# Softmax attention with another order of scores, maxima and values over two blocks of keys, and its first stacked rows fetched in four parts

## The chip, the cores and the metric

The kernel runs on one core of one Trainium2 chip. The metric is the device time of one execution in microseconds. Before the change, three executions took 3766.29, 3769.75 and 3779.08 us; the median is 3769.75 us.

## The reference, cut to what matters

The program is a network of six parts over x of shape (2, 2048, 256): a routed feed-forward part, a causal linear attention, the same feed-forward again, a feed-forward with 4-bit quantised operands, a softmax attention, and the quantised feed-forward again. Only the softmax attention is touched:

```
x = x + _L1_attn_ref(_layernorm(x, axis=-1), L1_attn_W_qkv, L1_attn_W_o)

b, n, _ = x.shape                     # 2, 2048, 256; 16 heads of 16
qkv = (x @ W_qkv.T).reshape(b, n, H, DH).transpose(0, 2, 1, 3)
score = softmax(einsum('bhif,bhjf->bhij', qkv, qkv) / 4, axis=-1)
attn = einsum('bhij,bhjf->bihf', score, qkv)
out = attn.reshape(b, n, F) @ W_o.T
```

Query, key and value are the same projection. Every row of scores has 2048 keys, and there are 2 x 16 x 2048 such rows.

## The kernel before, in words

The softmax attention is the function `attn1` (line 1492). Every engine walks through one generator, `plan()` (line 1554), that yields steps in one order, and does of each step its own share: TensorE (PE) the products, ScalarE (ACT) the exponentials and copies, VectorE (DVE) the maxima, normalisation and divisions, SyncE (SP) the DMAs. So the order of `plan()` is the order in which each engine issues, and an engine that waits for one step holds up all its later ones.

**Units and blocks.** A unit `u` is one batch row, one group of four heads and 512 queries; there are 32 (`UNITS`), four to a group of heads. Within it the loop `jt` goes over 16 blocks of 128 keys. Per block, `score` (line 1720) multiplies keys by queries for each of the four heads: a product of 50 rows into a ring of three PSUM banks `st`. Heads 0 and 2 lie on partitions 0 to 49 and heads 1 and 3 on 64 to 113, so that neighbouring products can use different halves of PE's rows. ACT takes the exponential (line 1796) into `PR`, a ring of two blocks. Score `s` waits until the exponential of `s - 2`, counted from one, is done: that is the one three places before it. The step `pv` (line 1734) multiplies the four exponentials of a block by the values, into bank `po`. It is issued one block late.

**Maxima.** A softmax needs the row's maximum first. The step `max` (line 1701, `m` in the order) computes scores with queries on the partitions, 48 rows, alternately on the two halves, into one of four spare banks, and DVE reduces it (line 1836). A unit has 64 of them (`MPU`), and they run 16 (`LEAD`) ahead of the unit's scores, so that unit `u + 1`'s last maxima fall in block 11 of unit `u`. Then the step `extremes` follows: DVE reduces once more (line 1843), PE transposes (line 1708), DVE splits into two parts (lines 1851 and 1853), and SP writes them out and reads them back as two more rows of the queries' tile `QS` (lines 1652 and 1656). The unit's first score waits for that.

**The order in a block** is the list `ORDER` (line 1508): `m s0 s1 m s2 v m s3 m`. After it come, outside the list:
- in block 0, `end` of the last unit: ACT copies `po` (line 1803), for which the first `pv` of the new unit waits, in block 1;
- in block 1, `tail` of the last unit: four transposes on PE (line 1742), and on DVE a reciprocal and a product (lines 1860 and 1864);
- from block 1 on, one step of `aside` per block. For units 1 to 4 these are the projection steps of the second batch row, 14 for each 512 rows: `norm` (DVE, line 124) and `turn` (PE transposes, line 1676, which wait for `norm`) four times by turns, `parts` twice (lines 1683, 1782, 1828) and `value` four times (line 1690);
- from block 2 on, one step of `put` per block, in the seven units 13 to 16 and 29 to 31: `ao` (PE transposes, line 1749, then an ACT copy, line 1811) and `wo` (line 1757, which waits for that copy, then DVE adds to x and takes the row's statistics), four times by turns.

**The start.** `project_steps(0)` projects the first batch row in four groups of 512 rows. Each group's parts go to DRAM (`q_parts`, line 1632). When all are there, the step `stack` (line 1640 on) reads them back as the stacked rows `KS` and `QS` of the first four heads, with 12 DMAs of 256 KB, and the first maximum waits for all of them. Stacks 1 to 7 are fetched in the same way while earlier units run. Before the first score come 80 steps `max`.

Of the kernel before, what the change touches and what calls it, by code (L numbers as in the profile page):

```python
# [6 lines left out]
F32 = mybir.dt.float32  # L7
# [49 lines left out]
def build_program(nc, A):  # L57
# [3 lines left out]
    TB = L // P  # L61
# [8 lines left out]
    DH = D // NH  # L70
    GT = 4
    G = T // GT
    GW = GT * P
# [5 lines left out]
    with ExitStack() as ctx:  # L79
        known = {}  # L80

        def event(name, by=1):
            if name not in known:
                known[name] = Event(ctx.enter_context(nc.semaphore(name)), by)
            return known[name]
# [1406 lines left out]
        def attn1():  # L1492
            with ExitStack() as scope:
                NPT = 3
# [3 lines left out]
                HG = 4  # L1498
                NPR = HG // 2
                NG = NH // HG  # L1500
                IC = L // GW
# [3 lines left out]
                UNITS = nb * NG * IC  # L1505
                SPU = TB * HG
                MPU = HG * GT * IC
                ORDER = ("m s0 s1 m s2 v m s3 m").split()
                LEAD = MPU // 4
                XN, XT = ring(scope, "sxn", [P, D], 2), sb("sxT", [P, KD, GW], scope=scope)  # L1510
                PART = ring(scope, "spart", [P, 2, GW], 2, F32R)
# [14 lines left out]
                part_out = [event(f"a1_part_out{i}", 16) for i in range(2)]  # L1526
                stack_in = [event(f"a1_stack_in{i}", 16) for i in range(2)]
# [6 lines left out]
                def project_steps(b):  # L1534

                    for g in range(IC):
                        for t in range(g * GT, (g + 1) * GT):
                            yield ("norm", b, t)
                            yield ("turn", b, t)
                        for o in range(KD):  # L1540
                            yield ("parts", b, g, o)
                        for t in range(g * GT, (g + 1) * GT):
                            yield ("value", b, t)

                def output_steps(u):
                    b, ic = u // (NG * IC), u % IC
                    for t in range(ic * GT, (ic + 1) * GT):
                        yield ("ao", b, t)
                        yield ("wo", b, t)

                def stacked(n):
                    return (n // 2 + 1) * 4 * NPT

                def plan():

                    yield from project_steps(0)
                    yield ("stack", 0)
                    for m in range(MPU + LEAD):
                        if m and m % MPU == 0:
                            yield ("extremes", m // MPU - 1)  # L1560
                        yield ("max", m)
                    m = MPU + LEAD
                    aside = iter(())
                    for u in range(UNITS):
                        b, g, ic = u // (NG * IC), u // IC % NG, u % IC
                        if ic == 0:
                            if g == NG - 1:
                                yield from aside
                            if u // IC + 1 < nb * NG:
                                yield ("stack", u // IC + 1)  # L1570
                        if (g, ic) == (0, 1) and b + 1 < nb:
                            aside = project_steps(b + 1)
                        put = output_steps(u - 1) if u and (u - 1) // IC % NG == NG - 1 else iter(())
                        for jt in range(TB):
                            j = u * TB + jt
                            for step in ORDER:
                                if step[0] == "s":
                                    yield ("score", j, int(step[1]))
                                if step == "v" and j:
                                    yield ("pv", j - 1)  # L1580
                                if step == "m":
                                    if m % MPU == 0 and m <= UNITS * MPU:
                                        yield ("extremes", m // MPU - 1)
                                    if m < UNITS * MPU:
                                        yield ("max", m)
                                    m += 1
                            if jt == 0 and u:
                                yield ("end", u - 1)
                            if jt == 1 and u:
                                yield ("tail", u - 1)  # L1590
                            if jt > 0:
                                yield from itertools.islice(aside, 1)
                            if jt > 1:
                                yield from itertools.islice(put, 1)
                        yield from put
                    yield ("pv", UNITS * TB - 1)
                    yield ("end", UNITS - 1)
                    yield ("tail", UNITS - 1)
                    yield from output_steps(UNITS - 1)

                use = {}
                for what in plan():
                    if what[0] in ("turn", "parts", "value", "extremes", "max", "tail", "ao", "wo"):
                        use[what] = len(use)
# [4 lines left out]
                def read(key):  # L1609

                    return pm_free[use[key] % 4](use[key] // 4 + 1)
# [4 lines left out]
                with nc.Block() as block:  # L1616

                    @block.sync
                    def _(e):
                        e.wait_ge(*fill_ok(1))  # L1620
                        for ks in KS:
                            for pr in range(NPR):
                                for i in range(2):
                                    e.dma_start(ks[HALF * i + KR:HALF * i + KM, pr, :].bitcast(F32).rearrange("p (c n) -> p c n", n=HALF),
                                                ones[:].bitcast(F32).unsqueeze(1).to_broadcast([2, L // HALF, HALF])).then_inc(*ones_in.up)
                        for what in plan():
                            kind, *at = what
                            if kind == "parts":
                                b, g, o = at
                                col = b * L + g * GW  # L1630
                                e.wait_ge(*read(what))
                                e.dma_start(parts[:, o * P:(o + 1) * P, col:col + GW].rearrange("s p n -> p s n"),
                                            PART[o][:].bitcast(F32)).then_inc(*part_out[o].up)
                            if kind == "stack":
                                n = at[0]
                                b, g = divmod(n, NG)
                                for o in range(KD):
                                    e.wait_ge(*part_out[o]((b + 1) * IC))
                                if n >= 2:
                                    e.wait_ge(*st_ok((n - 1) * IC * SPU))  # L1640
                                for dst, which in ((KS[n % 2], KEY), (QS[n % 2], QRY)):
                                    for j, part in enumerate(which):
                                        src = parts[part, g * HG * DH:(g + 1) * HG * DH, b * L:(b + 1) * L].rearrange(
                                            "(r i f) n -> i f r n", i=2, f=DH)
                                        for i in range(2):
                                            row = HALF * i + j * DH
                                            e.dma_start(dst[row:row + DH].bitcast(F32), src[i]).then_inc(*stack_in[n % 2].up)
                            if kind == "extremes":
                                u = at[0]
                                ic, n = u % IC, u // IC  # L1650
                                e.wait_ge(*read(what))
                                e.dma_start(maxima[u].rearrange("j r n -> r j n"), MB[u % 2][:].bitcast(F32)).then_inc(
                                    *max_in[u % 2].up)
                                e.wait_ge(*max_in[u % 2](3 * (u // 2) + 1))
                                for i in range(2):
                                    e.dma_start(QS[n % 2][HALF * i + KR:HALF * i + KM, :, ic * GW:(ic + 1) * GW].bitcast(F32).rearrange(
                                                    "j r (t n) -> j r t n", n=P),
                                                maxima[u].rearrange("j (r i t) n -> i j r t n", i=2, t=GT)[i]).then_inc(
                                        *max_in[u % 2].up)
# [234 lines left out]
        ffn0("b")  # L1894
        ffn1("a", False)
        attn1()
        ffn1("b", True)

# [23 lines left out]
```

## Time and profile before

| | |
|---|---|
| median of 3 executions | 3769.75 us |
| the profiled execution, its own time | 3781.05 us |
| its span, first to last instruction | 3779.3 us |
| PE busy | 3535.4 us, 94% |
| DVE busy | 2698.2 us, 71% |
| ACT busy | 2136.2 us, 57% |
| mean granted clock of PE | 0.953 |
| softmax attention, first transposes to the last `pv` | about 1836 to 3494 us |

Times in rows are in us from the span's start, and "mean ns" is one instruction. A row of the timeline gives start, duration, engine, line, operation and tiles; "x4" after it means that four neighbouring instructions are merged into one row, and the bracket is how long the engine sat idle before it and what released it. PE's matmuls are pipelined: the start in a row is when one is taken up, and its end is modelled. In this kernel one step `pv` shows as 8 matmuls of line 1734, and any other fp32 product as two for each that the code issues. PE's busy share is therefore not its share at peak: short waits lie hidden in it.

### The profile page before, as it was taken

Reading aid. Unit: us, or ns where it says so; the run is one execution under the profiler, and the core shown is the slowest. Engines: PE = TensorE matmul, PEld = TensorE weight load, DVE = VectorE, ACT = ScalarE, POOL = GpSimd, SP = SyncE. Lnnn points to the kernel's source line nnn. Section 1 sums busy time; section 2 is a strip of 40 time slices with the busy share of each in tenths; the row PEclk is TensorE's granted clock in tenths of the full one; section 3 lists DMA queues with packets and bytes.
Section 4 is the critical chain, followed back from the end, with each engine's and each line's share of the span. In section 5 each row is a group of like instructions: output and inputs, shape, how many; then the busy total and the mean of one; then the engine's idle time right before and its main releaser. Section 6 shows DMA issues by size and latency. Waiting matters only on the chain. (4 is left out here: it accounts for less than half of the span.)

```text
span 3779.3 us, 57424 instructions
## 1 busy us (share of the span) xinstructions
PE 3535.4 (94%) x22274; PEld 2399.2 (63%) x22274; DVE 2698.2 (71%) x4907; ACT 2136.2 (57%) x3830; POOL 600.5 (16%) x504
## 2 busy tenths in 40 slices
PE   6999998999799999799789999999999999999799
PEld 6888886777688888799534433333333333333798
DVE  4545544786454454799478888889889999882898
ACT  3444443443344444455327777777777777766555
POOL 4000001444400000355200000000000000000565
PEclk9999999999899999899969999899999999888899
DMA  3000001000200000000240211111021120000000
GB/s 116 1 1 1 1 1 40 2 2 1 72 1 1 1 1 1 1 1 1 64 50 13 46 24 21 16 20 17 9 28 14 22 28 8 2 2 1 6 18 23
DMA packets 34455, 63.93 MB, mean 17 GB/s; under 512 B 4309, under 2 KB 23433, under 8 KB 31113
## 3 DMA queue, kind: packets, MB, share of 16 engines
q1 hardware_dynamic: 34184, 60.27, 8.5%
q8 instruction: 177, 2.90, 0.3%
q14 instruction: 94, 0.76, 0.1%
HBM read 47.02 MB, written 13.11 MB: 16 GB/s over the span
## 5 line engine op out<-in xcount | busy, mean ns | idle before, releaser
L1836 DVE TENSOR_REDUCE smxp<-psum 128x1 f32<-128x512 f32 x2048 | 1276.3, 682 | 175.3 <-PE psum L1701 168.8
L1796 ACT ACTIVATE spr<-psum 128x512 f32<-128x512 f32 x2048 | 1082.3, 599 | 470.9 <-PE psum L1720 462.2
L1720 PE MATMUL psum<-sqs,sks 50*128 50x512 f32 x2048 | 754.6, 470 | 6.4 <-ACT spr L1796 3.1
L1701 PE MATMUL psum<-sks,sqs 48*128 48x512 f32 x2048 | 677.1, 457 | 29.5 <-DMA sqs<-q_parts 29.1
L1701 PEld LDWEIGHTS psum<-sks,sqs 48*128 48x128 f32 x2048 | 292.3, 198 | 538.7 <-issue 461.3
L1734 PE MATMUL psum<-spr,sv 128*32 128x512 f32 x4096 | 576.8, 636 | 1.8 <-ACT spr L1796 0.7
L1720 PEld LDWEIGHTS psum<-sqs,sks 50*128 50x128 f32 x2048 | 323.1, 194 | 200.9 <-ACT spr L1796 170.0
L1455 POOL MEMSET fhqb<- 128x64 f32 x3 | 0.3, 152 | 1668.9 <-POOLq L1616 1668.9
L389 PE MATMUL psum<-w2hi_a,hsa_hi 128*128 128x256 f32 x768 | 217.2, 283 | 16.8 <-DVE hsa_lo L531 16.8
L389 PE MATMUL psum<-w2hi_b,hsb_hi 128*128 128x256 f32 x768 | 217.3, 283 | 9.2 <-DVE hsb_lo L531 9.2
L389 PE MATMUL psum<-w2lo_b,hsb_hi 128*128 128x256 f32 x768 | 217.8, 284 | 0.0
L389 PE MATMUL psum<-w2lo_a,hsa_hi 128*128 128x256 f32 x768 | 217.7, 283 | 0.0
L389 PE MATMUL psum<-w2hi_a,hsa_lo 128*128 128x256 f32 x768 | 217.3, 283 | 0.0
L389 PE MATMUL psum<-w2hi_b,hsb_lo 128*128 128x256 f32 x768 | 217.3, 283 | 0.0
L525 DVE TENSOR_TENSOR hidb<-psum,maskb 128x512 f32<-128x512 f32 x128 | 88.3, 690 | 173.3 <-PE psum L355 173.3
L531 DVE TENSOR_TENSOR hsb_lo<-hidb,hsb_hi 128x512 fp32r<-128x512 f32 x192 | 147.3, 768 | 84.1 <-ACT hidb L444 75.8
L531 DVE TENSOR_TENSOR hsa_lo<-hida,hsa_hi 128x512 fp32r<-128x512 f32 x192 | 146.4, 763 | 83.8 <-ACT hida L444 75.4
L525 DVE TENSOR_TENSOR hida<-psum,maska 128x512 f32<-128x512 f32 x128 | 88.1, 688 | 158.9 <-PE psum L355 158.9
L447 ACT ACTIVATE hsb_hi<-hidb,b_b 128x512 fp32r<-128x512 f32 x128 | 92.6, 724 | 183.7 <-DVE hidb L525 183.7
L447 ACT ACTIVATE hsa_hi<-hida,b_a 128x512 fp32r<-128x512 f32 x128 | 92.7, 724 | 173.5 <-DVE hida L525 173.5
L1734 PEld LDWEIGHTS psum<-spr,sv 128*32 128x32 f32 x4096 | 82.9, 110 | 152.9 <-issue 126.5
L389 PEld LDWEIGHTS psum<-w2hi_a,hsa_hi 128*128 128x128 f32 x768 | 146.1, 190 | 28.2 <-DVE hsa_lo L531 20.5
(345 smaller groups left out, 7183.3 us busy)
## 6 DMA issues: line engine op xcount, KB each, us to landing
sks<-q_parts SPq DMA_DIRECT2D x48, 256.0 KB, 8.9
sqs<-q_parts SPq DMA_DIRECT2D x48, 256.0 KB, 20.0
q_parts<-spart SPq DMA_DIRECT2D x16, 512.0 KB, 2.7
x<-in_L_attn_x_dram SPq DMA_DIRECT2D x8, 512.0 KB, 7.3
rawa<-in_L_ffn_w_dram SPq DMA_DIRECT2D x16, 256.0 KB
rawb<-in_L_ffn_w_dram SPq DMA_DIRECT2D x16, 256.0 KB
out_dram<-x SPq DMA_DIRECT2D x8, 512.0 KB, 2.9
rawa<-in_L_ffn_sw_dram SPq DMA_DIRECT2D x8, 256.0 KB
```

What stands on the lines that cost most here:

```text
L389: m = e.matmul(ops[:, i // 2, (i % 2) * D:(i % 2 + 1) * D], hs[u][:, i * P:(i + 1) * P], w2[v][:, ex, c, :], start=(s == 0 and i % 2 == 0 ...
L447: e.activation(hi[:], hid[:], ACT.Relu, bias=bias).then_inc(*sc.up())
L525: e.tensor_tensor(HB[n % 2][:], psum[:, j % 3, :], mask[:, s // C0 - 1, :], ALU.mult).then_inc(*masked.up)
L531: e.tensor_tensor(lo[:], HB[n % 2][:], hi[:].bitcast(F32), ALU.subtract).then_inc(*low_ok.up)
L1455: m = e.memset(hq[:, H1:], 0.0)
L1701: e.matmul(bank(what), QS[n % 2][rows, pr, q0:q0 + P], KS[n % 2][rows, pr, jc * GW:(jc + 1) * GW], start=True, stop=True, tile_position=(H ...
L1720: e.matmul(st[s % 3], KS[n % 2][rows, pr, jt * P:(jt + 1) * P], QS[n % 2][rows, pr, ic * GW:(ic + 1) * GW], start=True, stop=True, tile_po ...
L1734: m = e.matmul(po[32 * hq:32 * hq + VW, :], VB[b][:, jt, c0:c0 + VW], PR[j % 2][:, hq, :], start=(jt == 0), stop=(jt == TB - 1), tile_posi ...
L1796: e.activation(PR[j % 2][:, hq, :], st[s % 3], ACT.Exp, scale=float(DH) ** -0.5).then_inc(*exp_ok.up)
L1836: e.tensor_reduce(out[:, r // (2 * GT * IC), r // (2 * IC) % GT, r // 2 % IC, r % 2:r % 2 + 1], bank(what), AX.X, ALU.max).then_inc(*pm_fr ...
```

## The change

It has three parts. The order is now over two blocks: `s0` to `s3` are the first block's scores and `s4` to `s7` the second's, the first `v` is the `pv` of the block before the pair and the second `v` that of the pair's first block. The `end` of the last unit comes after `s6` of the first pair, `tail` after that whole pair, and `aside` and `put` yield two steps after each of the other seven pairs, not one after each block. The first stack is fetched in four parts, each right after its group of the projection; in all 48 DMAs of 64 KB.

```diff
-                ORDER = ("m s0 s1 m s2 v m s3 m").split()
+                ORDER = ("s0 s1 m m s2 v s3 s4 m s5 m s6 m m m s7 v m").split()
...
                 def stacked(n):
-                    return (n // 2 + 1) * 4 * NPT
+                    return (n // 2 + (IC if n % 2 == 0 else 1)) * 4 * NPT
...
-                    yield from project_steps(0)
-                    yield ("stack", 0)
+                    for g in range(IC):
+                        yield from itertools.islice(project_steps(0), 14 * g, 14 * (g + 1))
+                        yield ("stack", 0, g)
...
-                        for jt in range(TB):
-                            j = u * TB + jt
+                        for jt in range(0, TB, 2):
+                            j, values = u * TB + jt, 0
                             for step in ORDER:
                                 if step[0] == "s":
-                                    yield ("score", j, int(step[1]))
-                                if step == "v" and j:
-                                    yield ("pv", j - 1)
+                                    yield ("score", j + int(step[1]) // HG, int(step[1]) % HG)
+                                if step == "v":
+                                    if j + values:
+                                        yield ("pv", j + values - 1)
+                                    values += 1
+                                if step == "s6" and jt == 0 and u:
+                                    yield ("end", u - 1)
...
                             if jt == 0 and u:
-                                yield ("end", u - 1)
-                            if jt == 1 and u:
                                 yield ("tail", u - 1)
                             if jt > 0:
-                                yield from itertools.islice(aside, 1)
-                            if jt > 1:
-                                yield from itertools.islice(put, 1)
+                                yield from itertools.islice(aside, 2)
+                                yield from itertools.islice(put, 2)
...
                             if kind == "stack":
-                                n = at[0]
+                                n, part_of = at
                                 b, g = divmod(n, NG)
+                                first, count = (0, IC) if part_of is None else (part_of, 1)
+                                cols = slice(first * GW, (first + count) * GW)
                                 for o in range(KD):
-                                    e.wait_ge(*part_out[o]((b + 1) * IC))
+                                    e.wait_ge(*part_out[o](b * IC + first + count))
...
-                                            "(r i f) n -> i f r n", i=2, f=DH)
+                                            "(r i f) n -> i f r n", i=2, f=DH)[:, :, :, cols]
...
-                                            e.dma_start(dst[row:row + DH].bitcast(F32), src[i]).then_inc(*stack_in[n % 2].up)
+                                            e.dma_start(dst[row:row + DH, :, cols].bitcast(F32), src[i]).then_inc(*stack_in[n % 2].up)
```

## Rows read from the trace of the kernel before

**Rows 1.** Timeline of one undisturbed block, PE, DVE and ACT

```profile
2889.96 1.06 PE L1734 MATMUL psum<-spr,sv 128*32 128x512 f32 x8
2890.95 0.49 PE L1701 MATMUL psum<-sks,sqs 48*128 48x512 f32 x1
2891.29 0.40 PE L1701 MATMUL psum<-sks,sqs 48*128 48x512 f32 x2
2891.48 2.48 DVE L1836 TENSOR_REDUCE smxp<-psum 128x1 f32<-128x512 f32 x4
2891.52 2.06 ACT L1796 ACTIVATE spr<-psum 128x512 f32<-128x512 f32 x4 [0.57 <-PE psum L1720]
2891.52 0.40 PE L1720 MATMUL psum<-sqs,sks 50*128 50x512 f32 x2
2892.17 0.50 PE L1720 MATMUL psum<-sqs,sks 50*128 50x512 f32 x1
2892.60 1.06 PE L1734 MATMUL psum<-spr,sv 128*32 128x512 f32 x8
```

**Rows 2.** Timeline around a step extremes, in block 12 of a unit

```profile
2905.79 1.07 PE L1734 MATMUL psum<-spr,sv 128*32 128x512 f32 x8
...
2908.64 0.22 DVE L1843 TENSOR_REDUCE smx<-smxp 128x16 f32<-128x64 f32 x1
2908.92 0.28 PE L1708 MATMUL psum<-ident,smx 128*16 128x128 f32 x1 [1.40 <-DVE smx L1843]
...
2910.01 1.07 PE L1734 MATMUL psum<-spr,sv 128*32 128x512 f32 x8
```

**Rows 3.** Timeline, the steps pv of a new unit's blocks 0, 1 and 2

```profile
2920.57 1.06 PE L1734 MATMUL psum<-spr,sv 128*32 128x512 f32 x8
...
2923.31 1.07 PE L1734 MATMUL psum<-spr,sv 128*32 128x512 f32 x8
...
2926.46 1.06 PE L1734 MATMUL psum<-spr,sv 128*32 128x512 f32 x8
```

**Rows 4.** Timeline of two blocks, one with ao and the next with wo

```profile
2743.02 0.44 PE L1749 MATMUL psum<-ident,sao 128*128 128x128 f32 x2
...
2743.49 0.38 ACT L1811 ACTIVATE saoT<-psum 128x256 f32<-128x256 f32 x1
...
2744.29 1.06 PE L1734 MATMUL psum<-spr,sv 128*32 128x512 f32 x8
...
2747.91 1.07 PE L1734 MATMUL psum<-spr,sv 128*32 128x512 f32 x8
```

**Rows 5.** Timeline of a block with turn, pv to pv, and a norm

```profile
2060.42 1.07 PE L1734 MATMUL psum<-spr,sv 128*32 128x512 f32 x8
...
2063.34 1.07 PE L1734 MATMUL psum<-spr,sv 128*32 128x512 f32 x8
...
2060.51 0.41 DVE L124 TENSOR_SCALAR sxn<-x,mv,rstd 128x256 f32<-128x256 f32 x1
```

**Rows 6.** Timeline of the first stack: its last six issues, and the first maximum

```profile
1879.15 2.75 SPq L1647 DMA_DIRECT2D sqs<-q_parts  x6
1904.77 0.50 PEld L1701 LDWEIGHTS psum<-sks,sqs 48*128 48x128 f32 x4 [29.48 <-DMA sqs<-q_parts]
```

**Rows 7.** Busy time by stretch: us, PE, PEld, DVE, ACT, POOL, PEclk, DMA share, GB/s

```profile
1882.00:1905.00 23.00, 0.23 (x2) 0.23 (x4) 0.00 (x0) 0.00 (x0) 0.00 (x0) 0.50 0.92 106
1957.00:3494.00 1537.00, 1489.32 (x8552) 593.63 (x8550) 1300.23 (x2228) 1118.62 (x2144) 0.00 (x0) 0.95 0.13 18
2800.00:3220.00 420.00, 404.23 (x2463) 158.86 (x2461) 388.81 (x652) 319.43 (x614) 0.00 (x0) 1.00 0.13 17
2287.00:2289.00 2.00, 2.00 (x9) 0.72 (x11) 1.64 (x4) 1.00 (x3) 0.00 (x0) 0.50 0.07 16
```

**Rows 8.** DMA issues: tiles, queue, count, KB each, median us to landing

```profile
q_parts<-spart SPq DMA_DIRECT2D x16, 512.0 KB, 2.7
```

**Rows 9.** Group of line 1803 in the softmax attention: busy us, mean ns

```profile
L1803 ACT ACTIVATE sot<-psum 128x512 f32<-128x512 f32 x32 | 18.9, 592 | 1.2 <-PE psum L1734 1.2
```

More of the change, by code:

```diff
@@ L1569, in plan @@
                             if u // IC + 1 < nb * NG:
-                                yield ("stack", u // IC + 1)
+                                yield ("stack", u // IC + 1, None)
                         if (g, ic) == (0, 1) and b + 1 < nb:
```

## The prediction

> **What bounds the kernel now.** I read the page's busy shares first (PE 94%), then the timeline of the softmax attention. It shows that PE's share hides waits. An undisturbed block runs from `pv` to `pv` in 2.64 us (2889.96 to 2892.60), and the same 2.64 comes back block after block [rows 1]. No engine is full in it: DVE's four maxima take 2.48, 0.60 apart with 0.68 for the first; ACT's four exponentials 2.06, after 0.57 of idle time. What ends last is a loop through two engines. `s3` stands behind `pv` and is taken up 1.00 after it; its exponential starts 0.57 later, and the next `s2` is taken up 0.65 after that (2891.52 to 2892.17), because the ring of three banks is then free; `pv` follows 0.43 later. 1.00 + 0.57 + 0.65 + 0.43 = 2.65. PE itself has about 0.4 to spare.
>
> PE's own price: after `pv` the first products cost 0.34 and each further pair, one product on each half of the rows, 0.23 (2890.95, 2891.29, 2891.52). I read that as a fill of 0.20 for a stretch of products, plus 0.23 for each pair; one alone before `pv` costs 0.43, as `s2` shows. The Trainium skill, "TensorEngine Tiling", section Key Properties, says that changing the tiling mode drains TensorE; the 0.34 against 0.23 agrees. By that rule alone, two steps of full height side by side would save a drain in each of the 56 pairs that have such steps, 0.20 x 56 = 11 us; by the rows the old drains lay in the loop's spare time, and nothing is saved.
>
> **The plain pair in the new order.** Let the first `v` start at 0; it ends at 1.00. Then come `s3 s4 | m s5 | m s6 | ...`, all alternating halves. `s3`'s exponential starts at 1.57, and `s6` needs it: it is taken up at 2.22. From there `s6`, `m m`, `m s7` are three pairs' time, 0.20 + 3 x 0.23 = 0.89, so the second `v` starts at 3.11. It needs the same exponential and does not wait. It ends at 4.11; `m s0 | s1 m | m s2` take 0.89, and the next `v` starts at 5.00. `s0`, `s1`, `s2` of the next pair need exponentials five, six and seven, spaced 0.52: 1.57, 2.08, ... the one of `s7` starts at 3.64 and releases at 4.29, before `s2` wants its bank. So two blocks take 5.00, against 5.28: a gain of 0.28 per plain pair. DVE needs 8 x 0.60 = 4.80, and is the floor for any better result: it takes up its maxima at 1.77 and works on to the sixth of them, the one after the second `v`, until about 5.45, some 0.8 after that product is there. This backlog matters below.
>
> **The steps beside the order.** In the old order a step of PE time X between two blocks makes the block 2.57 + X long (1.00, 0.67 for `m s3 | m`, X, 0.90 for the rest), as the `tail` block's 3.15 (2923.31 to 2926.46) [rows 3] and the `turn` block's 2.92 (2060.42 to 2063.34) [rows 5] show with X = 0.58 and 0.36; X is the row's duration less some 0.08. Since 0.4 us of the loop's slack is used up, the step costs only X - 0.07. In the new order PE is the bound where these steps stand, and the step also parts `m` from `s0`: 0.23 + 0.20 more. Cost there: X + 0.43, and any wait.
>
> - **`end`, `tail`** (31 pairs): ACT comes to `end` only after the exponential of `s6`, the fourth behind `s3`'s: at 1.57 + 4 x 0.51 = 3.62. The copy takes 0.59 [rows 9], and `pv` starts some 0.07 later: 4.28, not 3.11, which is 1.17. `tail` adds 0.58 + 0.43 = 1.01. The pair takes 7.18. In the old order the copy fell into ACT's idle 0.57: block 0 took 2.74 and block 1 3.15, together 5.89 [rows 3]. Loss 1.29 x 31 = **+40**.
> - **`extremes`** (31 pairs): DVE ends the last maximum at 5.45; reduction and transposition start bring it to 5.76 (2908.64 to 2908.92 [rows 2]). `s0` and `s1` have gone ahead, so only `m m | s2` follow: 0.21 + 0.66, `v` at 6.63. The old block took 4.22 (2905.79 to 2910.01) after one of 2.64, together 6.86. Gain 0.2 x 31 = **-6**. From the transposition to the next unit's first score there are then 9.9 us, for 10.6 before, with no wait for the read-back seen; if it needed all of the 10.6, this would cost up to 0.7 x 31 = 20.
> - **`norm`, `turn`** (16 pairs): they used to lie a block apart. Now PE comes to `turn` at 4.11 + 0.43 = 4.54, while DVE ends the maxima at 5.45 and `norm` (0.41 [rows 5]) at about 5.9; `turn` starts at 5.97. The pair ends at 5.97 + 0.36 + 0.89 = 7.22, the two old blocks took 2.64 + 2.92. **+27**. If DVE had no backlog the wait would be 0.6 at most, and this term 13 less.
> - **`ao`, `wo`** (28 pairs): ACT's copy starts 0.47 after `ao` and takes 0.38 [rows 4]. In the old order a block lies between; now `wo` waits from 4.90 to 5.46. 5.46 + 1.05 + 0.89 = 7.40, against 2.93 + 3.62 = 6.55 [rows 4]. **+24**; without the wait +8.
> - **`parts`, `value`** (12 pairs): both steps of a pair are ready, so the pair takes 5.00 + 0.43 + 2X, against 2.57 + X twice: 0.3 more whatever X is, **+3**.
> - **Plain pairs**: 256 less 31, 31, 28 and 28, plus 4 counted twice, is 142. 142 x -0.28 = -40. The granted clock over the stretch is 0.95 [rows 7], so a tenth of it ran at the lower of the two levels, 1.2 GHz, where PE is the bound and the orders hold the same products: **-36**.
>
> Sum of the orders: 40 - 6 + 27 + 24 + 3 - 36 = **+52 us**.
>
> **The first stack.** The first maximum starts at 1904.77, 29 us after PE had done the projection [rows 6]. The twelve DMAs are issued in 5.4 us (0.46 each, the last six in 2.75) and their 3 MB then drain at 106 GB/s with the DMA engines 92% busy [rows 7]. In four parts only the last quarter, 0.77 MB, is left when the projection is done: 7 us of draining from 1876.4 on, plus a landing of about 2.7 [rows 8]; say 1886. Three earlier parts, 5.5 us of issue and 7 of draining, fit in the 9.1 us from group to group, but SP issues the next group's write about a us late behind them, and it drains behind them; nothing on PE waits for that. Gain **-18.5**. Rows of 2 KB instead of 8 KB could drain more slowly. The write to `q_parts` also has 2 KB rows and lands 512 KB in 2.7, which speaks for the full rate; at half of it the gain is 11. The issue of 12 DMAs alone bars more than 22. The 80 maxima behind it are bound by DVE and unchanged. `stack` 1 to 7 are as before.
>
> **Forecast.** +52 - 18.5 = +33, about 3814 against the profiled execution's 3781, and 3803 against the median of 3769.75, which is 11 less. Its own range, from the bounds above, is 3783 to 3825.
>
> **Rivals.**
> 1. *The clock stays up.* At 44.4 us for an undisturbed unit (13 x 2.64 + 4.22 + 2.74 + 3.15), 32 units with 35 for the projection steps and 36 for `ao` and `wo` would make 1492; the stretch took 1537 [rows 7]. So 45 us went to stretches at 1.2 GHz. If the denser order kept 2.4 GHz throughout, -45 + 33 = -12: **3758, faster**. It decides once more than 33 of these 45 come back. For it: plain pairs idle 0.64 of 5.00 in one piece, not 0.4 of 2.64. Against: from 2800 to 3220 the old order held the full clock [rows 7], so it is not the plain block that loses it, and the waits behind `extremes` stay.
> 2. *The clock falls oftener.* The 2 us from 2287 on ran wholly at 1.2 GHz [rows 7], and before it PE had stood waiting for line 1843. The new waits, 1.2 before the new unit's `pv` and 1.4 before `turn`, are like the 1.40 before the old transposition [rows 2]. The Trainium skill, "TensorE: Matmul & The Clock Gate", section "HAM oscillation", says that idle gaps put the array back to half rate. If they cost half as much again as now, +22: **3825**.
> 3. *The alternation does not shorten the plain pair*, for instance if products of different halves do not overlap as I read it: 36 more, **3839**. Against: 0.23 per two products of 512 columns.
> 4. *The waits are hidden*: DVE without backlog, copies earlier than reckoned, -13, -16 and the `end` at half its price, -20: 3754. And the four parts may give nothing, because writes queue behind reads: 3821.
>
> **Chances.** Forecast 0.45; rival 1 0.12; rival 2 0.13; rival 3 0.08; rival 4 0.12 hidden and 0.10 without the fetch's gain. The range is 3757 to 3838. No change means within 0.3%, 3758 to 3781, about what a measurement of this kernel can tell. Faster: rival 1 in most of its cases and half of the hidden ones, 0.17. Same: the rest of these and the forecast's lower edge, 0.13. Slower 0.70.
>
> **What would show it.** Plain pairs: `pv` to `pv` 3.11 and 1.89 by turns, sum 5.00; ACT idle twice a pair. The first pair of a unit at 7.2, with `pv` waiting for line 1803. PE waiting for line 124 for 1.4 before `turn`, and for line 1811 for 0.6 before `wo`. First maximum at about 1886. A plain pair at 4.8 or at 5.3, a clock mean in the stretch other than 0.95, or no wait of `pv` for line 1803 would make it wrong.

## The result and the profile after

The changed kernel takes 3899.23 us (median of 4, 3877.97 to 3947.18), the kernel before 3774.41 (median of 4, 3766.29 to 3809.56): 1.029 of before, with an interval from 1.020 to 1.039. The forecast was slower, by 33 us; it became slower by 125. The sign and the steps reckoned at the full clock came out, the size did not, and the time lies far above the stated range of 3757 to 3838. One disturbed execution of the changed kernel, the 3947, is left out of the ratio, which is one of means and by which the change costs 111 us.

The profiled execution of the changed kernel has a span of 3908.8 us, against 3779.3. Its timeline has the same line numbers up to the order list; behind it `pv` is line 1739, `score` 1725, `max` 1706, the exponential 1801, the `end` copy 1808, `turn` 1681, `ao` 1754 and `wo` 1762.

An undisturbed pair in PE's and ACT's timeline, to be held against [rows 1]:

```profile
2381.40 1.07 PE L1739 MATMUL psum<-spr,sv 128*32 128x512 f32 x8
...
2382.93 2.55 ACT L1801 ACTIVATE spr<-psum 128x512 f32<-128x512 f32 x5 [0.24 <-PE psum L1725]
...
2383.58 0.50 PE L1725 MATMUL psum<-sqs,sks 50*128 50x512 f32 x1
...
2384.50 1.07 PE L1739 MATMUL psum<-spr,sv 128*32 128x512 f32 x8
...
2386.39 1.07 PE L1739 MATMUL psum<-spr,sv 128*32 128x512 f32 x8
```

3.10 and 1.89 by turns, 4.99 for two blocks, where 3.11, 1.89 and 5.00 were forecast; `s6` is taken up 2.18 behind the first `pv` (2.22 forecast). The pair with `extremes`, the first one of a unit, and one with `ao` and `wo` (PE's timeline again):

```profile
2389.49 1.06 PE L1739 MATMUL psum<-spr,sv 128*32 128x512 f32 x8
...
2393.02 1.06 PE L1739 MATMUL psum<-spr,sv 128*32 128x512 f32 x8
...
2639.47 1.06 PE L1739 MATMUL psum<-spr,sv 128*32 128x512 f32 x8
...
2642.56 1.06 PE L1739 MATMUL psum<-spr,sv 128*32 128x512 f32 x8
...
2643.99 0.44 PE L1754 MATMUL psum<-ident,sao 128*128 128x128 f32 x2
2644.90 1.13 PE L1762 MATMUL psum<-wo1T,saoT 128*128 128x256 f32 x4 [0.47 <-ACT saoT L1816]
...
2646.86 1.06 PE L1739 MATMUL psum<-spr,sv 128*32 128x512 f32 x8
```

2384.50 + 1.89 + 3.10 = 2389.49, then 3.53: 6.63 with `extremes`, as forecast. `ao` and `wo`: 3.09 + 4.30 = 7.39, forecast 7.40, with the wait for the copy in the bracket. So the steps reckoned at the full clock held. What it left out stands in the next rows, the new wait at a unit's start and what follows it, PE and ACT:

```profile
2402.99 1.07 PE L1739 MATMUL psum<-spr,sv 128*32 128x512 f32 x8
...
2406.44 0.63 ACT L1808 ACTIVATE sot<-psum 128x512 f32<-128x512 f32 x1
...
2407.17 1.94 PE L1739 MATMUL psum<-spr,sv 128*32 128x512 f32 x8 [1.02 <-issue]
2409.04 0.79 PE L1706 MATMUL psum<-sks,sqs 48*128 48x512 f32 x1
...
2412.38 1.93 PE L1739 MATMUL psum<-spr,sv 128*32 128x512 f32 x8
...
2417.29 1.94 PE L1739 MATMUL psum<-spr,sv 128*32 128x512 f32 x8
```

`pv` comes 4.18 after the one before it, as forecast, PE having stood idle for 1.02. But the `pv` that was waited for takes 1.94, not 1.07, and so do the next: 5.21 and 4.91 instead of 2.91 and 3.09. The view of busy time by stretch (PE, PEld, DVE, ACT, POOL, granted clock, DMA share, GB/s) says why, and shows how long it can last:

```profile
2397.00:2407.00 10.00, 8.97 (x60) 3.88 (x56) 9.77 (x17) 8.29 (x18) 0.00 (x0) 1.00 0.51 66
2407.00:2409.00 2.00, 1.83 (x8) 0.23 (x8) 0.85 (x2) 0.56 (x2) 0.00 (x0) 0.50 1.14 131
2409.00:2417.00 8.00, 8.00 (x32) 3.75 (x28) 3.97 (x8) 3.51 (x7) 0.00 (x0) 0.50 1.02 118
...
2643.00:2670.00 27.00, 24.75 (x142) 10.93 (x134) 21.27 (x42) 15.77 (x33) 0.00 (x0) 1.00 0.00 1
2685.00:2757.00 72.00, 68.39 (x240) 26.63 (x238) 38.86 (x70) 29.69 (x58) 0.00 (x0) 0.54 0.00 1
1940.70:3618.20 1677.50, 1561.13 (x8546) 632.70 (x8548) 1290.83 (x2227) 1102.59 (x2140) 0.00 (x0) 0.88 0.12 16
```

From full to half, that is 2.4 to 1.2 GHz, behind the wait, for 13.7 us by the granted clock. The other rows are two units of the same kind, each with its four pairs of `ao` and `wo`. The first (2643 to 2670) runs them at the full clock. In the second the clock has fallen at the unit's start and stays down through nearly the whole unit, 72 us; its pairs with `ao` and `wo` take 12.2 instead of 7.4. Over the whole stretch from the first `pv` to the last the granted clock is 0.88, where [rows 7] had 0.95.

How long PE was idle, and for whom, by total us, times and longest, in that stretch before and after:

```profile
PE psum L1708 <- DVE smx L1843: 39.3, 31, 1.4
PE psum L1720 <- ACT spr L1796: 3.1, 9, 0.5
```

```profile
PE psum L1739 <- issue: 31.3, 31, 1.0
PE psum L1713 <- DVE smx L1848: 24.5, 27, 1.0
PE psum L1681 <- DVE sxn L124: 18.8, 16, 1.4
PE psum L1762 <- ACT saoT L1816: 13.3, 28, 0.5
PE psum L1725 <- ACT spr L1801: 9.7, 42, 0.5
```

43 us in two kinds before, 98 in five kinds after. The 31 waits put down to "issue" are the 31 `pv` that stand behind the copy of line 1808. After the first unit the granted clock fell 14 times in the stretch: 11 times within half a us of that wait's end, 3 times within about a us of the end of a wait for `norm` (1.24 to 1.26 long), and never behind the 28 waits of 0.5 before `wo` or the 27 for line 1848. Before, it fell 15 times, each time within 2 us of the end of a wait for line 1843.

### The profile page after: what moved, and what is told of

Its sections match the earlier page's. It is cut to its first block and busy times, and to the rows that moved or that the text cites. A ratio compares the mean times of both kernels' runs of the same rounds, so it can differ in the third digit from the quotient of the medians.

```text
span 3908.8 us, 57463 instructions
## 1 busy us (share of the span) xinstructions
PE 3611.5 (92%) x22274; PEld 2440.0 (62%) x22274; DVE 2693.3 (69%) x4907; ACT 2122.4 (54%) x3830; POOL 598.6 (15%) x504
## 5 line engine op out<-in xcount | busy, mean ns | idle before, releaser
L1841 DVE TENSOR_REDUCE smxp<-psum 128x1 f32<-128x512 f32 x2048 | 1263.3, 681 | 251.0 <-PE psum L1706 235.1
L1801 ACT ACTIVATE spr<-psum 128x512 f32<-128x512 f32 x2048 | 1068.2, 603 | 500.3 <-PE psum L1725 499.0
L1706 PE MATMUL psum<-sks,sqs 48*128 48x512 f32 x2048 | 735.9, 466 | 11.7 <-DMA sqs<-q_parts 11.3
L1739 PE MATMUL psum<-spr,sv 128*32 128x512 f32 x4096 | 616.2, 677 | 31.3 <-issue 31.3
L1706 PEld LDWEIGHTS psum<-sks,sqs 48*128 48x128 f32 x2048 | 364.7, 205 | 299.3 <-issue 237.5
```

Of the source, the lines that this page charges most:

```text
L1706: e.matmul(bank(what), QS[n % 2][rows, pr, q0:q0 + P], KS[n % 2][rows, pr, jc * GW:(jc + 1) * GW], start=True, stop=True, tile_position=(H ...
L1739: m = e.matmul(po[32 * hq:32 * hq + VW, :], VB[b][:, jt, c0:c0 + VW], PR[j % 2][:, hq, :], start=(jt == 0), stop=(jt == TB - 1), tile_posi ...
L1801: e.activation(PR[j % 2][:, hq, :], st[s % 3], ACT.Exp, scale=float(DH) ** -0.5).then_inc(*exp_ok.up)
L1841: e.tensor_reduce(out[:, r // (2 * GT * IC), r // (2 * IC) % GT, r // 2 % IC, r % 2:r % 2 + 1], bank(what), AX.X, ALU.max).then_inc(*pm_fr ...
```

## The experiments

All times are medians. The ratio is one of means, to the kernel before, run on the same chip in the same job, with its 95% interval. The runs come from several jobs; so where a kernel is said to take some us less than the change, that is the difference of the two ratios times 3774. "Stretch" is the time from the first to the last `pv` in the profiled execution. That one execution took 9 to 35 us more than the median for the change, e2, e3, e6, e9 and e10, and 14 less for e8.

| kernel | us | ratio to before | stretch | clock in it |
|---|---|---|---|---|
| before | 3774 | | 1535.8 | 0.95 |
| changed | 3899 | 1.029 (1.020 to 1.039) | 1677.5 | 0.88 |
| e1 fetch alone | 3751 | 0.992 (0.988 to 0.995) | 1519.5 | 0.96 |
| e2 end early | 3766 | 0.996 (0.992 to 1.001) | 1549.5 | 0.94 |
| e3 steps apart | 3756 | 0.994 (0.990 to 0.998) | 1559.7 | 0.94 |
| e4 both | 3683 | 0.974 (0.969 to 0.980) | 1449.8 | 1.00 |
| e5 waits filled | 3759 | 0.998 (0.995 to 1.000) | 1527.2 | 1.00 |
| e6 old order, late end | 3851 | 1.023 (1.019 to 1.028) | 1618.9 | 0.91 |
| e7 late extremes | 3649 | 0.969 (0.965 to 0.972) | 1416.0 | 1.00 |
| e8 old order, no wait | 3686 | 0.979 (0.975 to 0.984) | 1441.3 | 1.00 |
| e9 only pv's wait filled | 3814 | 1.011 (1.005 to 1.018) | 1589.4 | 0.94 |
| e10 only the others filled | 3829 | 1.016 (1.011 to 1.022) | 1620.3 | 0.92 |
| e11 order alone | 3885 | 1.032 (1.028 to 1.035) | 1632.1 | 0.91 |

The theory was rival 2 of the prediction, at a greater price: PE's new waits let its clock fall. The rival to it was that the new order itself, by its products, loses the clock.

**e1, the fetch alone**, in the old order: the `stack` edits of the change, without the rest of its diff.

> The kernel before with the first stack fetched in four parts, and its old order. Both theories: the first maximum 17 us earlier, nothing else, 0.9955 of before (3757). If it is not below 0.998, the parts cost something behind the start that the trace of the change hides.

3750.52 against 3778.60, 28 less, and the interval reaches from 0.988 to 0.995, so the 17 (0.9955) lie just outside its edge. In its trace the first maximum starts at 1888.2, 16.6 earlier than in [rows 6]. The start gains what was reckoned; whether the rest is more than the spread of the old order's clock is not settled.

**e2, the end early:**

```diff
-                                if step == "s6" and jt == 0 and u:
+                                if step == "s4" and jt == 0 and u:
                                     yield ("end", u - 1)
```

> The changed kernel with the step end after s4, not after s6: the copy comes two exponentials earlier, so the new unit's first pv waits 0.16, not 1.1 us. At the full clock that is 1.0 x 31 = 31 us less than the changed kernel (0.992 of it). Theory waits (PE's new waits let the clock fall, and what it costs comes on top): the dips right behind the wait for line 1808, in every second unit, go too, 60 to 80 less, about 3825, 1.014 of before. Rival order (the new order itself, by its denser products, runs at the low level more often, waits or not): 31 less only, about 3868, 1.025 of before.

3765.54, 124 less than the change, of which the moved copy explains 31. The time was missed downward, past the theory's own figure, and the rival's 3868 is out. In this trace the first pair of a unit takes 3.20 + 2.91 from 2275 on, unit after unit, with no dip behind it. The units 1 to 4, with `turn` and its wait, are another matter; granted clock in the two parts of the stretch:

```profile
1994.00:2275.00 281.00, 261.91 (x1089) 104.59 (x1081) 164.35 (x280) 141.96 (x279) 0.00 (x0) 0.70 0.14 27
2275.00:3480.00 1205.00, 1140.98 (x7095) 476.22 (x7094) 1070.54 (x1866) 910.98 (x1769) 0.00 (x0) 1.00 0.12 15
```

With the copy out of the way, the `turn` units still run at a low level, and 28 waits of 0.5 before `wo` leave the clock at 1.00. How the clock falls behind a `turn` wait shows in the changed kernel's own PE timeline, in unit 2, nine us behind the copy's wait:

```profile
2062.78 1.07 PE L1739 MATMUL psum<-spr,sv 128*32 128x512 f32 x8
2065.51 0.66 PE L1681 MATMUL psum<-ident,sxn 128*128 128x128 f32 x2 [1.24 <-DVE sxn L124]
2067.68 1.93 PE L1739 MATMUL psum<-spr,sv 128*32 128x512 f32 x8
```

The granted clock was 1.00 up to 2065 and 0.50 from 2067 on. In e2, which has hardly a wait for the copy, the clock falls within 2 us of a `turn` wait's end in each of the units 1 to 4.

**e3, the steps apart:**

```diff
                             for step in ORDER:
+                                if step == "s6" and jt > 0:
+                                    yield from itertools.islice(aside, 1)
+                                    yield from itertools.islice(put, 1)
...
                             if jt > 0:
-                                yield from itertools.islice(aside, 2)
-                                yield from itertools.islice(put, 2)
+                                yield from itertools.islice(aside, 1)
+                                yield from itertools.islice(put, 1)
```

> The changed kernel with the two steps beside the order set apart: the first before s6, where PE waits anyway, the second at the pair's end. The waits of turn for norm and of wo for its copy go, 1.43 x 16 + 0.8 x 28 = 45 us at the full clock. Theory waits: the pairs with ao and wo no longer stay at 1.2 GHz from the first to the last, 90 or more less than the changed kernel, about 3805. Rival order: 45 less, about 3854.

3755.87, 133 less than the change, of which 45 were reckoned at the full clock. The pair with `ao` and `wo` takes 3.54 + 3.38 = 6.92, not 7.39. The dips behind the copy's wait are still there in many units; two of the four units with projection steps stay down through most of their length after one (0.63 from 2037 to 2106), though they have no wait for `norm` any more. Of the seven units with `ao` and `wo` only the last had a dip, over three intervals of `pv`.

**e4, both edits:**

> Both of these edits in the changed kernel. At the full clock 76 less than the changed kernel, about 27 less than before. Theory waits: the clock's mean is back at 0.95 or above and the time at 3735 to 3750, 0.990 to 0.995 of before, below both kernels. Rival order: 3823, 1.013 of before, with a mean clock near 0.92.

3682.86, 0.974 of before: better than the 0.990 expected at most, and its four executions lie within 4 us (3680.63 to 3684.63), where e1 and e2, with dips, spread over 47 and 51 in ten. The clock is at 1.00 from the first `pv` to the last. A unit without side steps takes 42.65. Together the two edits take 208 off, 76 of them by the reckoning at the full clock. Its waits for the last reduction before `extremes`, 27 of at most 1.0, are those of the change.

**e5, the waits filled.** This kernel keeps every step of the change in its place and adds products that nobody reads:

```diff
+                            if kind == "fill":
+                                u, count = at[:2]
+                                free(what)
+                                for i in range(count):
+                                    m = e.matmul(bank(what), QS[u // IC % 2][0:KR, 0, 0:P], KS[u // IC % 2][0:KR, 0, 0:GW],
+                                                 start=True, stop=True, tile_position=(0, 0))
...
+                                    if jt == 0 and u and values:
+                                        yield ("fill", u, 4, "end")
...
+                                    if side[0] == "turn":
+                                        yield ("fill", u, 5, side)
...
+                                    if side[0] == "wo":
+                                        yield ("fill", u, 2, side)
```

> The changed kernel, order and all, with useless products put into PE's three new waits: four of line 1706's form before the new unit's first pv, five before each turn, two before each wo (their results go to a spare bank and are not read). Theory waits (PE standing still lets its clock fall): more work in less time, mean clock in the softmax attention back near 1.0 and 3760 to 3780, about 1.00 of before, since e4_both and the 76 us of waits put it there at the full clock. Rival order or work: the added products cost time or nothing, 3895 or more, 1.03 of before, and the clock stays at 0.92.

3759.25, 120 less than the change with 260 products more. Where the change had its wait, PE's timeline now has this:

```profile
2395.37 1.06 PE L1756 MATMUL psum<-spr,sv 128*32 128x512 f32 x8
...
2398.49 1.19 PE L1726 MATMUL psum<-sks,sqs 48*128 48x512 f32 x4
2399.60 1.07 PE L1756 MATMUL psum<-spr,sv 128*32 128x512 f32 x8
...
2402.52 1.06 PE L1756 MATMUL psum<-spr,sv 128*32 128x512 f32 x8
```

`pv` comes 4.23 after the one before it, no earlier than in the change, and it takes 1.07. The stretch at a glance, this kernel's and then e4's:

```profile
1941.70:3468.90 1527.20, 1465.80 (x8810) 624.42 (x8808) 1284.21 (x2227) 1099.34 (x2140) 0.00 (x0) 1.00 0.13 18
```

```profile
1942.90:3392.70 1449.80, 1397.70 (x8548) 579.84 (x8548) 1284.17 (x2227) 1097.19 (x2140) 0.00 (x0) 1.00 0.13 19
```

This is the experiment that decides. The order, every wait for data and ACT's and DVE's work are the change's; only PE has something to do in them. 1527.2 is about what the change's order costs at the full clock; 1677.5 is what it took. The fillings have a price of their own, an estimate of some 10 us: a filled pair with `ao` and `wo` takes 4.42 + 3.09 = 7.51, not 7.39, a filled `pv` comes 0.05 later, and three short dips are left (at the starts of units 18, 25 and 31). So the 77 between e5 and e4 is the price of the waits themselves, reckoned at 76, and these 10; that the two figures agree is in part luck.

**e6, the wait in the old order:**

```diff
                             for step in ORDER:
+                                if step == "s1" and jt == 1 and u:
+                                    yield ("end", u - 1)
...
-                            if jt == 0 and u:
-                                yield ("end", u - 1)
```

> The kernel before, old order and one fetch, with end issued after s1 of the new unit's second block: its copy comes two exponentials later and the first pv waits about 1.1 us, as in the change. At the full clock +1.0 x 31 = 31 us (1.008 of before). Theory waits: dips right behind line 1803's wait as in the change, so clearly more than 31: +60 to +100, 1.016 to 1.026. Rival order (only the new order loses its clock): 1.008 and a mean clock of 0.95 as before.

3850.58 against 3768.86: 82 more, for 31 at the full clock. PE and ACT in the trace:

```profile
2269.67 1.06 PE L1734 MATMUL psum<-spr,sv 128*32 128x512 f32 x8
...
2272.69 0.60 ACT L1803 ACTIVATE sot<-psum 128x512 f32<-128x512 f32 x1
...
2273.39 1.69 PE L1734 MATMUL psum<-spr,sv 128*32 128x512 f32 x8 [1.01 <-DVE smxp L1836]
...
2278.09 1.07 PE L1734 MATMUL psum<-spr,sv 128*32 128x512 f32 x8
```

The same wait, and a slow `pv` behind it (1.69, then 4.70 to the next, for 3.15 in [rows 3]), with an order that has nothing of the change. The bracket names DVE's last event, but what `pv` waits for is the copy of line 1803, which starts 0.70 before it. The rival is out from this side too. But the 51 us beyond the 31 don't all lie behind the new wait: of 27 falls of the clock in this trace 7 come behind it, and 20 behind the old order's own wait for line 1843, where the kernel before had 15.

**e7, late extremes**, on top of e4: the step is kept back when its maximum is reached and issued before the next `s3`.

```diff
+                                if step == "s3" and late:
+                                    yield ("extremes", late.pop())
...
                                     if m % MPU == 0 and m <= UNITS * MPU:
-                                        yield ("extremes", m // MPU - 1)
+                                        late.append(m // MPU - 1)
```

> e4_both with the step extremes two maxima and a pv later, before s3, when DVE has finished the unit's maxima: the last long wait of PE in a unit, 1.4 us for line 1848, goes. The pair of 6.62 falls to 5.2 to 5.4, 31 of them give 37 to 43 us: 3640 to 3646, 0.989 of e4_both. The clock is at 1.0 there already and gives nothing more in either theory. If the read-back of the maxima comes too late for the next unit, the gain is eaten by a wait of its first score.

3648.99, 34 less than e4 by the medians and by the stretches, against 37 to 43. The pair takes 3.48 + 1.90 = 5.38, for 6.62, and no first score waits for the read-back. This version beats both kernels, by 120 us (0.969, 0.965 to 0.972) and by 230.

**e8, the old order without its wait:** e1 with `extremes` kept back to the `v` of its block.

> The old order with the fetch in four parts and extremes moved behind pv: the old order without PE's one long wait. At the full clock 1.3 x 31 = 40 us below e1_fetch_alone, 0.989 of it, 0.981 of before. Theory waits: the 45 us that the old order lost at 1.2 GHz go too, 0.97 of before, and the clock in the stretch is 1.0. Rival order: about 0.981, clock 0.96.

3686.27, 0.979 of before, and less than e1 by 64 in the medians and 47 by the ratios. That lies between the two figures, and the rival's 0.981 is inside the interval, so the time does not tell them apart; the clock does: 1.00 in the stretch, where e1 has 0.96, with no fall at all. That holds for the profiled execution, the fastest of the four; the others took 14 to 20 us more at a lower mean clock (0.968 to 0.970 over the whole kernel, for 0.975), so they did not keep it throughout. The old order's own dips came in the main from its one long wait. Its block with `extremes` takes 2.84, for 4.22 in [rows 2]. Against it e7, with the same fetch and the same full clock, is 37 us faster by the medians and 25 by the stretches: the 25, both at the full clock, is about what the alternation over two blocks is worth once its waits are gone.

**e9 and e10, one kind of filling each:** of e5's edit only the four products before `pv`, or only those before `turn` and `wo`.

> The changed kernel with useless products in one kind of wait only, the four before the new unit's first pv; the waits of turn and wo stay as in the change. Theory each wait starts its own low stretches: the dips behind line 1808 go, those of units 1 to 4 with turn stay: about 100 us less than the change, near 3800. Rival, only the sum of waits counts: the clock gains in proportion, 31 x 1.1 of 31 x 1.1 + 16 x 1.4 + 28 x 0.6 = 74 us of waits, so half of the 140 that e5_filled_waits gave: near 3830.

> The changed kernel with the products in the other waits, five before each turn and two before each wo, none before pv. Each wait its own: dips of 1.5 to 6 us behind line 1808 stay in every second unit, but no pairs with ao and wo run at 1.2 GHz to the end: about 100 less than the change, near 3800. Rival, only the sum of waits counts: 70 less, near 3830.

3813.70 and 3829.02, 68 and 49 less than the change, where e5 had 120. e10 lands on the rival's figure, the share of the waiting time that is filled; e9 lies between the two, and its interval (3790 to 3836) holds both. The two gains nearly add up to e5's, and neither kind of wait alone is most of the loss.

The traces fit neither theory whole. In e10 all ten falls come behind the unfilled wait of `pv`. In units 14 and 30 the low level then lasted through all pairs with `ao` and `wo` (4.92 + 7.93 = 12.85 for each), although their waits were filled; the first theory had said that no such pairs would. In e9 three falls come behind `turn`'s wait, but three more at a unit's start, where the wait was filled, and one of these lasted through unit 16 (81.5 us for 53.3). How a single wait's length turns into time at 1.2 GHz stays open.

**e11, the order alone:** the change with `stack` in its old form.

> The changed kernel with its first stack fetched at once, as before: the change without its fetch. Both parts of the change are far apart in time, so 17 us more than the change: about 3915, 1.034 to 1.040 of before, with a mean clock near 0.92. If it is no slower than the change, the fetch in four parts gave nothing in this order.

3885.37, by the ratios 8 us more than the change, where 17 were expected; its first maximum starts at 1906.0, 18 later. The interval (1.028 to 1.035) lies inside the change's (1.020 to 1.039), so the two can't be told apart. In the one profiled execution each, its stretch has a clock of 0.91 against 0.88, and that outweighs the start. As a measure of the fetch the run is inconclusive.

## Why the prediction was wrong

**The frame.** From the first `pv` to the last the change took 141.7 us more in the profiled executions; before it the start gained 16.7, and behind it 4.5 were lost: 129.5, the difference of the spans. The ratio's 111 is 18 less, since the change's profiled execution took 18 us more than the mean behind the ratio; the sums below are those of the profiled executions.

**The steps at the full clock: right.** Plain pair 5.00, measured 4.99. Pair with `extremes` 6.63 and 6.63. First pair of a unit 7.18 and 4.18 + 2.91 = 7.09. `ao` and `wo` 7.40 and 7.39. `norm` and `turn` 7.22 and 3.09 + 4.00 = 7.09, where the clock was up. A pair of `value` steps, at 5.00 + 0.43 + 2 x 1.05 = 7.53, took 7.34. Summed over the stretch: the old order at the full clock is e8's 1441.3 and 31 x (4.22 - 2.84) for the wait that e8 removes, 1484; the change's is e5's 1527.2. The difference is 43, forecast 52; without the 10 us of e5's own it is nearer 35.

**The fetch: right.** -18.5 forecast, -16.9 for the first maximum (1887.88 after 1904.77). SP's rows show where the rest went:

```profile
1876.27 0.94 SPq L1635 DMA_DIRECT2D q_parts<-spart  x2
1880.54 2.65 SPq L1652 DMA_DIRECT2D sks<-q_parts  x6
1883.24 2.75 SPq L1652 DMA_DIRECT2D sqs<-q_parts  x6
1887.88 1.22 PE L1706 MATMUL psum<-sks,sqs 48*128 48x512 f32 x4 [11.33 <-DMA sqs<-q_parts]
```

The last write was issued behind the third part's twelve reads, and the last reads began at 1880.54, not 1876.4: the prediction had such a write "about a us late" with "nothing on PE" waiting for it, but it came over 3 us later than before, and the first maximum waited. In return the reads were through 1.9 after the last issue. In these 7.4 us the DMA engines were 41% busy at 106 GB/s, where the old fetch had them 92% busy at the same rate, so they were not what limited a part; whether issue or landing did is not shown.

**The step that failed: the clock, held at its old loss.** The forecast carried the old order's 45 us at 1.2 GHz over unchanged ("a tenth of it ran at the lower of the two levels", -36 instead of -40) and gave rival 2, more dips from the new waits, +22 and a chance of 0.13. Measured: the change lost 1677.5 - 1527.2 = 150 us to the low level, the old order 1535.8 - 1484 = 52. That is 98 more, not 22, and with 43 for the orders it is the 141. (With e5's own 10 us taken off, the clock's part is that much larger and the orders' that much smaller.) e5 shows the cause and e6 shows that it doesn't need the new order. Rival 2 was the right mechanism; its price was set at "half as much again" without a working, while the idle time of PE went from 43 to 98 us, in more and other places. A low level can also last, which a sum over single waits misses: units with side steps that entered them low stayed down nearly whole (0.54 over 72 us), and came back in the pairs behind the last of these steps, or in those with `parts`; in units without such steps a dip ended within four intervals of `pv`. e3 shows such long stretches in projection units without the wait for `norm`, and e10 in units with `ao` and `wo` whose waits are filled, so waits alone don't explain how long a dip lasts; that stays open.

**A reading that was wrong:** rival 1 was held unlikely because "the waits behind `extremes` stay". e4 has those waits and a clock of 1.00: one wait of 1.0 in 42 us did no harm, where the old order's, of 1.4, did some (15 falls in 31 waits).

The Trainium skill, "TensorE: Matmul & The Clock Gate", section "HAM oscillation", tells of a clock that swings, for gaps longer than any here. By that section alone waits of 1.0 to 1.4 us would have cost no clock, and the time would have stayed near the forecast's 3803; here they did cost it, and the measurement decides. No run varied the length of one wait by itself.

## What to carry to other kernels

Before a step is moved behind another engine's result, count PE's idle time by waiter, before and after, and don't price new waits of about a us at their length alone: here 77 us of them drew some 100 more at the low clock, and in e6 31 us of them came to 82 in all. It is no fixed rate: 27 waits of 1.0 in e4 drew nothing, and the 28 of 0.5 in e2 neither. Two dependent steps on different engines should keep other work between them; and where a wait can't be removed, useless products in it are a cheap test of what the clock is costing, and sometimes a cure.

## What was not expected of the hardware

A kernel with 260 more products on its busiest engine was 120 us faster (0.998 of before against 1.029). Idle times of 1.0 to 1.4 us, none longer, were enough for a granted clock of 0.88 over 1.7 ms and, in e2, of 0.70 over 281 us, while in the same kernel waits of 0.5 and of 1.0 us over the next 1.2 ms left it at 1.00. The spread of a kernel's times was least where the clock kept its full level: 4 and 5 us over four executions for e4 and e7, 18 or more for every other kernel.
